# First layer of a decoder: one setup stage, quantising rows while projecting, queries and keys by pairs with the scores' maximum, and an end in two stages

## The reference

```python
def _pot_scale(x):                      # power of two from the largest absolute value
    m = jnp.maximum(jnp.max(jnp.abs(x)), 1e-08)
    return jnp.exp2(jnp.ceil(jnp.log2(m / 127.0)))
def fq_floor(x):
    s = _pot_scale(x); return jnp.clip(jnp.floor(x / s), -128.0, 127.0) * s
h = (x - mu) * rsqrt(var + 1e-5)
h = h * fq_round(ln_gamma) + fq_round(ln_beta)
qkv = fq_floor(fq_floor(h) @ fq_round(w_qkv))          # 512 -> 3 * 1024
q, k, v = split(qkv)                                    # 16 heads of 64
dots = fq_floor(einsum('bhnd,bhmd->bhnm', q, k) * temp)
attn = fq_floor(softmax(dots))
out = einsum('bhnm,bhmd->bhnd', attn, v)
out = fq_floor(fq_floor(out) @ fq_round(w_out))        # 1024 -> 512
x = _layernorm(x + out)
```

## Time and profile before

| what | value |
|---|---|
| median of 3 runs | 4758.8 us (4752.11 to 4759.27) |
| profiled execution | 4760.2 us, its span 4758.4 us |
| TensorE busy | 3473.4 us (73%) |
| VectorE busy | 2508.3 us (53%) |
| ScalarE busy | 1610.4 us (34%) |
| mean granted clock of TensorE | 0.853 |

### The profile page before, as it was taken

How to read it: one execution, slowest core, us unless ns; L and a number is a source line. 1 busy time by engine, 2 the same in 40 slices (tenths; PEclk the granted TensorE clock), 3 DMA queues, 4 the chain that set the end, 5 groups by cost and what they waited for, 6 DMA issues and landing times. The chain is left out here.

```text
span 4758.4 us, 73335 instructions
## 1 busy us (share of the span) xinstructions
PE 3473.4 (73%) x27204; PEld 2399.3 (50%) x27234; DVE 2508.3 (53%) x3545; ACT 1610.4 (34%) x2869; POOL 599.2 (13%) x373
## 2 busy tenths in 40 slices
PE   0299741119640899999999999986997099999990
PEld 0143421116410666666666666653554089898980
DVE  6766698879964244444444444433865133333335
ACT  0103309978510233333333333322322034333331
POOL 0000000000000122222222222221011400000004
PEclk9999855555575899999999999997998599999995
DMA  3030332223113100001100000103110323222207
GB/s 137 36 118 0 100 101 81 78 78 96 53 62 117 41 26 26 26 26 32 44 26 26 26 26 26 33 5 71 37 28 27 119 95 120 75 87 75 88 33 253
DMA packets 176506, 303.71 MB, mean 64 GB/s; under 512 B 76648, under 2 KB 76648, under 8 KB 172160
## 3 DMA queue, kind: packets, MB, share of 16 engines
q1 hardware_dynamic: 167296, 273.37, 18.5%
q0 software_dynamic: 8960, 26.58, 1.6%
HBM read 172.42 MB, written 100.93 MB: 57 GB/s over the span
## 5 line engine op out<-in xcount | busy, mean ns | idle before, releaser
L1409 DVE TENSOR_REDUCE arena<-psum 112x4 f32<-112x1504 f32 x256 | 441.4, 1724 | 770.5 <-PE psum L1239 770.4
L1153 POOL TENSOR_TENSOR arena<-arena 125x896 f32<-125x896 f32 x192 | 401.7, 2092 | 1261.9 <-ACT arena L1382 1261.9
L1382 ACT ACTIVATE arena<-psum 125x1792 f32<-125x1792 f32 x192 | 320.1, 1667 | 408.3 <-PE psum L1252 408.2
L559 PE MATMUL psum<-arena 64*112 64x224 bf16 x1024 | 127.3, 401 | 348.0 <-DVEq L668 261.2
L684 ACT ACTIVATE arena<-arena,scales 112x224 bf16<-112x224 int8 x512 | 286.0, 559 | 35.1 <-DVEq L669 35.0
L559 PEld LDWEIGHTS psum<-arena 64*112 64x112 bf16 x1024 | 81.8, 200 | 393.5 <-DVEq L668 283.6
L1239 PE MATMUL psum<-arena 32*112 32x376 f32 x2048 | 237.1, 533 | 53.3 <-ACT arena L1382 27.7
L421 PE MATMUL psum<-arena 128*128 128x512 bf16 x1104 | 251.3, 383 | 14.0 <-DVEq L473 8.2
L2153 PE MATMUL psum<-tokens_T_high,w_high 128*128 128x384 f32 (+1 forms) x768 | 255.7, 333 | 3.7 <-issue 2.1
L2155 PE MATMUL psum<-tokens_T_high,w_rest 128*128 128x384 f32 (+1 forms) x768 | 254.8, 332 | 0.0
L2154 PE MATMUL psum<-tokens_T_rest,w_high 128*128 128x384 f32 (+1 forms) x768 | 254.5, 331 | 0.0
(11 more groups left out here) (313 smaller groups left out, 7432.0 us busy)
## 6 DMA issues: line engine op xcount, KB each, us to landing
arena<-L_ffn_moe_w SPq DMA_DIRECT2D x16, 2048.0 KB, 11.9
arena<-arena SPq DMA_DIRECT2D x32, 896.0 KB, 5.3
arena<-ctx SPq DMA_DIRECT2D x16, 1500.0 KB
rows_by_slot<-arena SPq DMA_DIRECT2D x1, 17920.0 KB, 49.3
arena<-x SPq DMA_DIRECT2D x2, 7168.0 KB, 22.4
arena<-x_after_attn SPq DMA_DIRECT2D x32, 448.0 KB, 15.3
dots_ints<-arena SPq DMA_DIRECT2D x16, 784.0 KB, 4.8
arena<-dots_ints SPq DMA_DIRECT2D x16, 784.0 KB, 5.6
```

The source lines that it names most:

```text
L559: last = PE.matmul(psum[0:HALF, 4 * (hg % 2) + j, half * NS:(half + 1) * NS], stage[at, u, h // 2, half * HALF:(half + 1) * HALF], stage[a ...
L1153: G.tensor_tensor(pair2[:, t, :, :], prob[:, t, :, 0:NS], prob[:, t, :, NS:2 * NS], ALU.add).then_inc(paired, 1)
L1382: S.activation(prob[:, t, :, :], score_psum(MC, 2 * NS), ACT.Exp, scale=SCALE2).then_inc(exp_done, 1)
L1409: return V.tensor_reduce(rmx[:, i // 2, i % 2, :], score_psum(HALF, HC), axis=AX.X, op=ALU.max).then_inc(r_free, 1)
```

## The change

- Setup: the phases `wl`, `wq`, `ln` and their scales become one phase `s1`. The small loads come first, x comes in seven chunks and w_qkv in four. ScalarE normalises the tiles and casts the levels of the weights; VectorE does the rest.
- Phase `hq` holds quantising, transposing and the products for the maximum. The order is by blocks of 512 rows: eight sets of three column groups (12 products, three banks), with one row tile of the next block after every second set. The loops are written out.
- Phase `qd` holds the products of q and k and the scores for the maximum, by pairs of heads: a piece of the next pair's products (up to 1024 rows), then the scores of two batches of this pair, straight from `qk`. It takes the place of `qq` and `dm`.
- End: phase `ow` makes levels and products by chunks of 512 rows and takes the maximum from PSUM, keeping nothing. Phase `yl` makes the products again, quantises from PSUM, adds x, takes the statistics, normalises on ScalarE and stores, all by chunks.

```diff
+            with phase(nc, "s1", ...) as (...), nc.Block() as block:
                 @block.sync
                 def _(sp):
-                    sp.dma_start(X[:, :, :], x_d.rearrange("(t p) d -> p t d", p=P)).then_inc(x_in, 16)
                     sp.dma_start(gb[:, 0, :], a["L0_attn_ln_gamma"].partition_broadcast(P)).then_inc(g_in, 16)
...
+                    for i in range(NCH1):
+                        sp.dma_start(X[:, chunk(i), :], x_d.rearrange("(t p) d -> p t d", p=P)[:, chunk(i), :]).then_inc(x_in[i], 16)
+                    for k in range(KC):
+                        sp.dma_start(qkvw[:, k, :], ...).then_inc(w_in[k], 16)
...
                 @block.scalar
                 def _(act):
+                    act.wait_ge(scale_ready, 1)
+                    for i in range(NCH1):
+                        for t in range(i * LG, (i + 1) * LG):
+                            done = S.activation(X[:, t, :], X[:, t, :], ACT.Identity, bias=stat[:, t, 5:6], scale=stat[:, t, 2:3])
+                        done.then_inc(normed, 1)
+                    for k in range(KC):
+                        act.wait_ge(w_levelled, k + 1)
+                        S.copy(qkvw_q[:, k, :], lv[:, k % 2, 0:3 * IN1]).then_inc(w_cast, 1)
...
+                    def scaled(i):
+                        dve.wait_ge(normed, i + 1)
+                        x = X[:, chunk(i), :]
+                        ch.link(V.tensor_tensor(x, x, gbq[:, 0, :].unsqueeze(1).broadcast_to([P, LG, D]), ALU.mult))
+                        ch.link(V.tensor_tensor(x, x, gbq[:, 1, :].unsqueeze(1).broadcast_to([P, LG, D]), ALU.add))
+                        ch.link(V.tensor_reduce(part[:, 8 + i:9 + i], x, axis=AX.XY, op=ALU.max, apply_absolute_value=True))
...
+                def in_order(rows_of, set_of):           # phase hq, VectorE and TensorE
+                    for t in range(LG):
+                        rows_of(t)
+                    for j in range(NBLK):
+                        for i in range(SETS):
+                            set_of(j, i)
+                            if i % 2 == 1 and j + 1 < NBLK:
+                                rows_of((j + 1) * LG + i // 2)
...
+                    def rows_of(n):                      # VectorE
+                        if n >= 2:
+                            dve.wait_ge(h_ready, n - 1)
+                        V.tensor_scalar(lv[:, n % 2, :], X[:, n, :], col("i_h"), FLOOR, ALU.mult, ALU.add).then_inc(levelled, 1)
+
+                    def set_of(j, i):
+                        m = j * SETS + i
+                        dve.wait_ge(mm_done, m + 1)
+                        at = 2 + OCS * (m % 2)
+                        V.tensor_reduce(part[:, m:m + 1], psum[:, at:at + OCS, :], axis=AX.XY, op=ALU.max, ...).then_inc(max_taken, 1)
...
+                    for n in range(TT):                  # ScalarE: ints(n) casts, moved(n) copies to hT
+                        ints(n)
+                        if n % LG >= 1:
+                            moved(n - 1)
+                        if n % LG == LG - 1:
+                            moved(n)
...
+                    def set_of(j, i):                    # TensorE
+                        m = j * SETS + i
+                        if i == 0:
+                            pe.wait_ge(hT_ready, j * LG + LG)
+                        if m >= 2:
+                            pe.wait_ge(max_taken, m - 1)
+                        for c in range(OCS):
+                            oc = i * OCS + c
                             for k in range(KC):
+                                last = PE.matmul(psum[:, 2 + OCS * (m % 2) + c, :], qkvw_q[:, k, oc * P:(oc + 1) * P], hT[:, k, j * D:(j + 1) * D], ...)
+                        last.then_inc(mm_done, 1)
...
+            def in_order(products_of, dots_of):          # phase qd, VectorE and TensorE
+                for m in range(UN):
+                    products_of(m)
+                for p in range(NPAIR):
+                    for i in range(UN):
+                        if p + 1 < NPAIR:
+                            products_of((p + 1) * UN + i)
+                        for b in range(i * NB // UN, (i + 1) * NB // UN):
+                            dots_of(p, b)
...
+                    def dots_of(p, b):                   # TensorE
+                        d = p * NB + b
+                        if b == 0:
+                            pe.wait_ge(moved, p * UN + UN)
+                        if d >= 2:
+                            pe.wait_ge(max_taken, d - 1)
+                        for half in range(2):
+                            for j in range(2):
+                                ...
...
+                    for c in range(NCH1):                # phase ow, VectorE
+                        rows = slice(c * LG * P, (c + 1) * LG * P)
+                        if c >= 1:
+                            dve.wait_ge(oq_ready, c)
+                        V.tensor_scalar(lv[:, :, :], oT[:, :, rows], col("off_o"), col("c_o"), ALU.add, ALU.mult).then_inc(levelled, 1)
+                        dve.wait_ge(levelled, c + 1)
+                        V.tensor_copy(oq[:, :, rows], lv[:, :, :]).then_inc(oq_ready, 1)
+                        if c >= 1:
+                            largest(c - 1)
+                    largest(NCH1 - 1)
...
+                    for i in range(NCH1):                # phase yl, VectorE
+                        tiles = range(i * LG, (i + 1) * LG)
+                        for t in tiles:
+                            dve.wait_ge(mm_done, t + 1)
+                            V.tensor_scalar(ylv[:, t % LG, :], psum[:, t % 8, :], col("off_y"), col("c_y"), ALU.add, ALU.mult).then_inc(y_read, 1)
+                        dve.wait_ge(y_read, (i + 1) * LG)
+                        dve.wait_ge(x_in[i], 16)
+                        for t in tiles:
+                            done = V.scalar_tensor_tensor(X[:, t, :], ylv[:, t % LG, :], col("s_y"), X[:, t, :], ALU.mult, ALU.add)
...
+                        if i >= 1:
+                            scales(i - 1)
```

More of the change, by code:

```diff
@@ L328, in decoder_kernel @@
[L328 to L333, removed]
+                    act.wait_ge(var_done, 1)
+                    S.activation(stat[:, :, 1], stat[:, :, 7], ACT.Sqrt, bias=col("eps"), scale=1.0).then_inc(std_done, 1)
+                    act.wait_ge(scale_ready, 1)
[3 more added lines that the diff above has]
+                        done.then_inc(normed, 1)
@@ L365, in _ @@
                     ch.link(V.tensor_copy(p, t8[:, 3:4]))
-        with ExitStack() as st:
[L369 to L378, removed]
+                    dve.wait_ge(w_cast, KC - 1)
@@ L464, in _, with products_of @@
                 @block.tensor
                 def _(pe):
-                    with pe.Fori(0, 2 * IN1 // P) as oc:
-                        for g, (lo, hi) in enumerate(GROUPS):
-                            pe.wait_ge(bank_free, oc * 2 + g + 1)
-                            qkv_products(pe, oc, lo, hi).then_inc(mm_done, 1)
+                    def products_of(m):
+                        oc, (lo, hi) = piece(m)
+                        if m >= 2:
+                            pe.wait_ge(lv_ready, m - 1)
+                        for k in range(KC):
+                            for j in range(lo, hi):
+                                last = PE.matmul(psum[:, 2 * (m % 2) + j - lo, :], qkvw_q[:, k, oc * P:(oc + 1) * P], hT[:, k, j * D:(j + 1) * D],
+                                                 start=(k == 0), stop=(k == KC - 1))
+                        last.then_inc(mm_done, 1)
@@ new lines, in dots_of @@
+                    def dots_of(p, b):
[5 more added lines that the diff above has]
+                        for half in range(2):
+                            for j in range(2):
+                                at = slice(DH1 * j, DH1 * (j + 1))
+                                rows = slice(b * NS + half * HALF, b * NS + (half + 1) * HALF)
+                                last = PE.matmul(psum[0:HALF, 4 + 2 * (d % 2) + j, half * NS:(half + 1) * NS], qk[at, p, rows],
+                                                 qk[at, NPAIR + p, b * NS:(b + 1) * NS], start=True, stop=True)
+                        last.then_inc(d_mm, 1)
@@ L907, in _ @@
+                    dve.wait_ge(var_done, NCH1)
+                    scales(NCH1 - 1)
                 @block.scalar
                 def _(act):
-                    act.sem_inc(kept, 2)
-                    with act.Fori(0, TT // 2) as pair:
-                        i = pair * 2
-                        for u in range(2):
-                            act.wait_ge(mm_done, i + u + 1)
-                            S.copy(Y[:, bass.ts(i + u, 1), :].rearrange("p a d -> p (a d)"), psum[:, u, :]).then_inc(kept, 1)
@@ L945, in decoder_kernel @@
+                    for i in range(NCH1):
+                        act.wait_ge(var_done, i + 1)
```

(4 more changed lines are left out.)

421 lines of the change are left out of this document (229 added, 192 removed).

## The result

The changed kernel takes 4733.4 us (median of 6 runs, 4723.5 to 4736.0) against 4757.7 for the kernel before (6 runs, 4752.1 to 4759.3): ratio 0.9946, 95% interval 0.9936 to 0.9956. That is 24 us faster; 4730 was forecast. The profiled execution took 4726.8, its span is 4724.7.

A forecast was written before the change was run, and what follows sets the result against it. It took different engines to bound different first-layer stages, with everything after 1502 us only shifting. Terms -62 + 91 - 15 - 44 = -30 against 4760.2 gave 4730 us; range 4682 to 4784, the forecast's own range 4710 to 4752.

The forecast's parts named there:

- A: Start of first layer, one setup stage: ends at 128 us instead of 190.5, 62 saved, bounds 56 to 68.
- B: Quantising while projecting, phase `hq`: 281 us against 189.9 before, 91 lost, bounds 51 to 122.
- the transposes hide: Rival for phase `hq`: transposes hide as the order intends, stage 165 us, kernel 4614; chance 0.03.
- full clock 250: Phase `hq` with TensorE at full clock throughout: 250 us, 60 lost.
- The stop: Phase `hq`: TensorE stands still 3.25 us at each of 24 row tiles, awaiting maximum, levels and cast.
- The clock: Phase `hq`: four stops in five bring half clock, each costing half of 3 us; 31 us over 24 stops.
- the lower bound of 51 for B: Least loss given for quantising while projecting, 51 us; the clock's own lower bound there was 0.
- the upper bound: Clock's largest cost in phase `hq`: every one of 24 stops falls, 2.6 us each, 62 us.
- C: Pair stage `qd`: 209 us at full clock, 222 with partial half clock and boundary; 15 saved, bounds 27 saved to 6 lost.
- D: End of first layer in two stages of 57 and 87 us: 44 saved, bounds 36 to 50.
- The clock holds: Rival: full clock through `hq` stops and `qd` steps, stages 250 and 209 us, kernel 4687; chance 0.27.
- Half clock for nearly the whole pair of sets: Rival: after each of 24 row tiles in `hq`, half clock costs 2.6 us, 62 in all; kernel 4782; chance 0.18.

The follow-up runs named there:

- without the stops: Kernel after with only VectorE's list changed in the stage of products: each row tile's levels written two sets earlier; 4627.4 us, ratio 0.9729.
- busy stops: Kernel after with 13 overwritten 128x512 matmuls on TensorE in each of the 24 stops, ahead of the wait for ScalarE's cast; 4680.0 us, ratio 0.9840.
- paired tiles: Kernel after with row tiles taken two at a time, after sets 4 and 8 of a block, giving 12 stops instead of 24; 4676.6 us, ratio 0.9837.
- the busy piece: Kernel after with the half-size fourth piece's products made twice for each q or k column block in the pair stage; 4702.3 us, ratio 0.9880.

## Why the prediction came out as it did

**A.** Forecast 128 and 62 saved; the stage ends at 128.3, and undoing it moves the end of the first layer by 64. Right by its own steps too: x's first chunk is taken up at 12.3 us (forecast 12), the first scaling starts at 39.6 (forecast 40).

**B.** Forecast 281, measured 275.9. The mechanism is the one that was read out of the list: without the stops 164.9, and the rival that the transposes hide gave 165 for that case. By parts: full clock 250 forecast, 239.6 measured with busy stops. The stop was mis-sized: TensorE is idle for 2.90 us where 3.25 was forecast, 8 of the 10 us, since the handovers are shorter than taken (0.04 from the last product to the maximum, and the levels start before the maximum has ended). The clock was taken as 31, and was 36.3: all 24 stops fall, not four in five, and each costs 1.5 us. The working had slips that cost little: four in five times half of 3 us is 1.2 a stop, 29 and not 31, and the lower bound of 51 for B doesn't follow from its terms, which give 60.

The Trainium skill, TensorE: Matmul & The Clock Gate, section "HAM oscillation — how this bites in real kernels", says that waits between bursts bring the half rate back in each turn of a loop. In the kernel after the trace agrees on the "each": all 24 stops fell. The run with paired tiles does not: 8 of its 12 did, with the same 2.90 us of idle. What it cost was 36 of the 62 us of the upper bound, since full clock was back after about 3.4 us.

**C.** Forecast 209 at full clock and 12 for the clock; measured 207.7 with the busy piece (clock 0.95, the falls between the pieces gone) and 15.5 for those falls, 223.2 in all. VectorE is busy 201.3 of 223.2 us, 90%, and its maxima take 1.08 us. Right.

**D.** Forecast 57 and 87; measured 56.2 and 85.2, 47 saved where 44 was forecast.

**The step that failed** is one sentence: "Everything after 1502 us is left as it is, so it shifts by the sum". The sum was -30, the first layer's shift is -36.8, and the whole came to -24.3. All that lies behind the first layer gave back 12.5 of it by the medians (3255.7 us from the second layer's first load on before, 3268.2 after). In the profiled executions the loop is 10.3 longer, but what lies behind the loop is 8.0 shorter, so that their spans differ by 33.7; that 8.0 is discussed below. The runs with 64 and 256 more instructions, one without the second pauses and one with them, show that the longer loop comes from its place in TensorE's program, and from no state that the first layer leaves. So 4730 was hit in part because a first layer forecast 7 us too slow met a loss of 12 that nobody had priced. Without that loss the kernel stands at 4718.7, still within the forecast's own range.

**The rivals.** "The clock holds" (4687) is out: the half clock was there at each stop. With busy stops, where it holds in B but still falls in C, the kernel is at 4680; 14 us of that are the loop's, so it is no test of the 4687. "Half clock for nearly the whole pair of sets" (4782) had the place right but not the price: it needed 2.5 us a stop, and 1.5 came. "The transposes hide" (4614) was no property of the order as written; VectorE's list, changed by itself, gives it: 4627.

What stays open: why the second pause needs just this place, and what decides whether a stop of 2.90 us is followed by half clock. Behind the loop the profiled executions take 1517.6 to 1528.2 us from kernel to kernel, with the same code, which I can't assign; the 8.0 between before (1525.6) and after (1517.6) is part of that.

## What to carry to other kernels

Where two engines walk the same written order, look at what one of them makes *for* the other: it must be issued earlier on the maker's list than it is used on the user's. Here moving one line two sets ahead is worth 106 us, more than the whole change. Price a short stop of TensorE as the stop plus the half clock that can follow it (3.1 + 1.5 us here, where it followed each time); if the stop must stay, throwaway matmuls in it give the second part back. And when a part is undone to learn its worth, read it at the end of its own stage: the total can move by 10 to 14 us because code further down has slid in the program.

## What the runs showed of the hardware that was not expected

A loop that nobody touched became 10 to 15 us longer when the code in front of it on TensorE had another length: at each of the six returns to its start a second pause of 0.7 to 2.1 us, shortly behind the usual one of 2.6 to 3.2. Moved by 64 instructions the pause went, moved by 256 it came back. The Trainium skill, Runtime: NRT & Kernel Launch, section "Instruction fetch mechanics", says that instructions are refilled in blocks of 256 and that a taken branch to a block that isn't at hand stalls the engine; that the pause is back after 256, and stands where the loop returns, agrees with that. That a loop's start 1 instruction further shows no second pause (in the kernel before) it does not explain.

The half clock behind a short stop need not show in the stop itself. At the stop shown above the clock is 1.00 to 154.0 us and 0.51 from there, after an idle time from 150.9 to 153.8; over the 24 stops the fall comes between 0.1 us before and 0.4 us behind the moment at which TensorE resumes. In a longer idle time it comes in the midst of it: in the kernel before at 1526.4, after the last matmul at 1523.9. Nor does each stop of this length bring it: of the 12 stops with paired tiles, four had full clock behind them. And two stretches of added, useless work on TensorE made the kernel faster: 13 matmuls in each stop (36 us of stage B) and 4 in each short piece (15.5 us of stage C).
